# A transformer layer whose 1,450-word step table is written in a new order

## What is computed

```
mod = (silu(c) @ wmod)                      # six vectors of 256 for each batch element
h = layernorm(x) * (1 + ca) + sa
x = x + ga * attn(h)                        # 16 query heads in 4 groups, rope, causal softmax
h = layernorm(x) * (1 + cb) + sb
x = x + gb * ffn(h)

attn(h):  q, k, v = h@Wq+bq, h@Wk+bk, h@Wv+bv; scores = q k^T / sqrt(16), masked; y = softmax(scores) v
          return y @ Wo + bo                # the four query heads of a group are summed into one
ffn(x):   routed = sigmoid(x @ w_router + b_router) > 0.5
          h = x + (rmsnorm(x) @ wv + bv) @ wo
          mlp = (silu(h2 @ w_gate) * (h2 @ w_up)) @ w_down    # h2 = rmsnorm(h), 704 inner columns
          return where(routed, h + mlp, x)
```

## Time and profile before

| | us |
|---|---|
| median of three runs | 466.64 (465.21 to 467.13) |
| span of the profiled execution | 466.8 |
| TensorE busy | 437.2 (94%) |
| TensorE loading weights | 371.8 (80%) |
| VectorE busy | 353.9 (76%) |
| ScalarE busy | 308.4 (66%) |
| GpSimd busy | 182.2 (39%) |

### The profile page before, as it was taken

How to read it: one execution, slowest core, us unless ns; L and a number is a source line. 1 busy time by engine, 2 the same in 40 slices (tenths; PEclk the granted TensorE clock), 3 DMA queues, 4 the chain that set the end, 5 groups by cost and what they waited for, 6 DMA issues and landing times. The chain is left out here.

```text
span 466.8 us, 9486 instructions
## 1 busy us (share of the span) xinstructions
PE 437.2 (94%) x3320; PEld 371.8 (80%) x3320; DVE 353.9 (76%) x796; ACT 308.4 (66%) x640; POOL 182.2 (39%) x262
## 2 busy tenths in 40 slices
...
GB/s 192 333 93 51 3 97 1 2 1 3 0 3 11 43 2 0 2 70 1 27 86 24 2 1 24 1 26 5 20 51 9 24 22 2 25 1 24 22 25 46
DMA packets 16576, 16.04 MB, mean 34 GB/s; under 512 B 4233, under 2 KB 14926, under 8 KB 16530
## 3 DMA queue, kind: packets, MB, share of 16 engines
...
## 5 line engine op out<-in xcount | busy, mean ns | idle before, releaser
L792 PE MATMUL banks<-gTh,guhi 128*128 128x256 f32 x352 | 101.2, 287 | 0.0
L794 PE MATMUL banks<-gTh,gulo 128*128 128x256 f32 x352 | 98.8, 281 | 0.0
L793 PE MATMUL banks<-gTl,guhi 128*128 128x256 f32 x352 | 98.7, 280 | 0.0
L937 ACT ACTIVATE PT<-banks 128x1024 f32<-128x1024 f32 (+3 forms) x96 | 74.5, 810 | 29.8 <-PE banks L708 24.4
L792 PEld LDWEIGHTS banks<-gTh,guhi 128*128 128x128 f32 x352 | 66.4, 189 | 1.6 <-issue 0.7
L1165 DVE TENSOR_REDUCE mxp<-banks 128x2 f32<-128x1024 f32 (+3 forms) x56 | 61.9, 1141 | 6.4 <-PE banks L684 3.9
L793 PEld LDWEIGHTS banks<-gTl,guhi 128*128 128x128 f32 x352 | 66.5, 189 | 0.3
L794 PEld LDWEIGHTS banks<-gTh,gulo 128*128 128x128 f32 x352 | 66.4, 189 | 0.0
L684 PE MATMUL banks<-QKT 128*128 128x512 f32 (+3 forms) x192 | 49.9, 368 | 6.8 <-ACT QKT L915 3.4
L708 PE MATMUL banks<-QKT 128*128 128x512 f32 (+3 forms) x192 | 50.9, 369 | 0.9 <-ACT PT L937 0.4
L708 PEld LDWEIGHTS banks<-QKT 128*128 128x128 f32 x192 | 30.3, 190 | 23.3 <-issue 21.2
...
## 6 DMA issues: line engine op xcount, KB each, us to landing
...
```

What stands on the lines that cost most here:

```text
L792: pe.matmul(out_, guhi[:, k, blk, :], gh, start=(m == 0 and k == 0), stop=False)
L793: pe.matmul(out_, guhi[:, k, blk, :], gl, start=False, stop=False)
L794: i = pe.matmul(out_, gulo[:, k, blk, :], gh, start=False, stop=(m == len(blocks) - 1 and k == KB - 1))
L937: act.activation(PT[:, u % 2, 2 * q:2 * q + 2, 0:CH - q0], both("prob", b, n)[:, :, 0:CH - q0], ACT.Exp, scale=float(D) ** -0.5).then_inc( ...
```

## The change

Only the string `ORDER` differs. Its words are the same, as many of each, in another sequence, and TensorE words have other bank digits, which changes the waits for free banks. No instruction is added or removed. Of the table's 58 lines the first two:

```
-ldx ldx ldx ldx pzero asetw stats setw pmodc vmodc rstd1 norm1 norm1 xT4 xev qkv5 stats norm1 norm1 xT4 xev qkv4 asetb
-setb pmod amod rstd1 norm1 norm1 xT6 xev norm1 norm1 xT7 qkvb qkvb rope pprep0 afwv vkeys sthi qkv6 xev aprep pprep1
+ldx ldx ldx ldx pzero vkeys asetw stats pmodc setw rstd1 asetb norm1 stats norm1 norm1 xT4 norm1 vmodc xT5 setb rstd1
+xev qkv4 norm1 norm1 pmod xev qkvb norm1 norm1 pprep0 amod qkv5 afwv gmod xT4 qkvb xT3 xev rope qkv4 aprep pprep1
```

113 lines of the change are left out of this document (57 added, 56 removed).

## The result

The new order takes 471.99 us (470.19 to 474.56, 4 runs) against 466.44 (465.21 to 467.13): 1.0131 times the time before, 95% interval 1.0095 to 1.0166. I had forecast 464.5 us and a range up to 469.0.

A forecast was written before the change was run, and what follows sets the result against it. TensorE bounds it behind 160 us, VectorE's maxima from 36 to 60, cross-engine chains from 60 to 140. 466.8 + 0.0 (start) + 0.0 (maxima) - 2.5 (element 1) + 0.0 + 0.5 (full TensorE) - 0.3 (tail) = 464.5 us; range 461.0 to 469.0.

The forecast's parts named there:

- The base: Starting figure of the sum: the profiled 466.8 us, left uncorrected because span and median (466.64) differ by less than runs do.
- The start, 0.0: Up to the first `stack`: moving `vkeys` ahead wins and loses nothing; 0.0 us, bounds -0.5 and +1.0.
- does not take the first transposes before 13.62: At the start: the TensorE begins transposes only at 13.62, so it sees less of the 3.95 us delay; transposes 0.9 later.
- wrong if the first `stack` comes after 33 us: Sign set beforehand, at the start: a first `stack` later than 33 us would show the forecast wrong.
- Maxima of element 0, 0.0: Row maxima and what follows, up to 86 us: later `prob0.8` (+1.5) nearly all comes back; 0.0, bounds -1.0 and +1.5.
- Element 1, -2.5: From 86 us to element 1's maxima: shorter TensorE pauses, maxima at 98.0 instead of 100.52; -2.5 us, bounds -0.5 and -3.8.
- Where the TensorE is full, +0.5: Behind 160 us: too little TensorE work between some dependent steps makes pauses; +0.5 us, bounds -1.5 and +2.5.
- the four places that I named: Behind 160 us: pauses ahead of `prob2.8`, `prob2.0`, `yT2.0` and `up3.6`, 2.5 us, of which 0.5 was there before.
- The tail, -0.3: At the end: `fin3.2` begins 0.5 us earlier, out of the way of VectorE's L1286; -0.3 us.
- (A): Rival: element 1's whole chain (-3.8) and filled pauses (-1.2) count, nothing lost where TensorE is full; 461.8 us, chance 0.24.
- (B): Rival: VectorE takes up element 1's gain, and later `prob0.8` adds 1.5; 466.5 us, chance 0.20.
- (C): Rival: thin start lowers the clock (+1.7), late transposes +0.5, element 1's gain lost; 469.5 us, chance 0.14.

The follow-up runs named there:

- old_vfirst: The kernel before with one move alone, `vkeys` (three memsets on VectorE) put right behind `pzero`: 470.45 us, 1.0078 times the kernel before.
- old_light: The kernel before with GpSimd's `fin` steps (but the last pair's) and `ffl` from the third pair on cut to 8 columns, wrong values: 463.79 us, 0.9937.
- after_again: The changed kernel, unaltered, run once more for a second profile: 471.53 us, 1.0100 times the kernel before.

## Why the prediction was wrong, by its own steps

- **The base.** I set a span against a median of run times. A run takes 1.7 to 1.9 us more than its span, so the profile shown is of an execution of about 468.5 us, 1.9 above the median. Put right, the same sum gives 464.5 + 1.7 = 466.2 counted from that execution, but 466.4 - 2.3 = 464.1 counted from the median.
- **The start, 0.0: wrong, +5.7** to `stack0.0` by the medians of eight traces each (29.0 and 34.7), of which the maxima give 1.8 back, so +3.9. The first step that failed is that the TensorE "does not take the first transposes before 13.62". That is the profile's late `pmodc`; in the usual execution they start at 10.4 to 11.6, and `vkeys` ahead of them then costs what old_vfirst shows, 4.0 us. The second is "the first `stack` starts at about 31.7", followed along the TensorE's own queue through `pprep1`. In the new order `stack0.0` waits for VectorE's `stlo0.0`: `vkeys` (by way of `xT0.0`, 14.14) and `vmodc` (15.08) both keep `xev0.0` until 15.39, `pmod` holds `qkv0.1` (which the sum counted as a pause filled), and `rope0.0`, `qkvb0.2` and `stats1.0` follow. `stats0.0` came at 9.47 (forecast 9.8), `xT0.0` at 14.14 (14.5), `stack0.0` at 33.07 (31.7), and in the other traces of this front at 34.0 to 35.5; "wrong if the first `stack` comes after 33 us" was met.
- **Maxima of element 0, 0.0: better than forecast.** From `stack0.0` to `a0.0` the new order, with `vkeys` at the top, takes 48.3 to 48.6 us, the old one 50.1 to 50.5. `prob0.8` came late as traced, at 67.50 (67.2 to 67.4), and that cost nothing in the end.
- **Element 1, -2.5: right in sum, partly by luck.** -2.6 in every trace. `qkv1.3` started at 93.35 (forecast 92.7) and `max1.0` at 98.02 (98.0). But I took the maxima's gain as 98.0 against VectorE's 100.52, the start of a matmul against that of a reduction. The first reduction came at 99.39, 1.1 earlier; the gain up to `prob1.0` is 1.9, and 0.7 more falls between `prob1.0` and `down0.0`, which I had put at 0.0. TensorE timeline of after:

```profile
93.35 1.54 PE L663 MATMUL banks<-Wqkv,xTc 128*128 128x192 f32 x8
94.72 2.02 PE L673 MATMUL banks<-ident,stk 128*128 128x128 f32 x16
98.02 0.56 PE L684 MATMUL banks<-QKT 128*128 128x128 f32 x4
```

- **Where the TensorE is full, +0.5: wrong, +4.9** (the back's 4.5 without the tail). I weighed TensorE work against the length of chains and took each VectorE step at its usual length. Of the four places that I named only `prob2.8` shows the wait, 0.3 us; the waits that count end at VectorE. What I left out is how much VectorE and GpSimd work the new order puts side by side: between 283.5 and 326.4 us VectorE is busy for 38.0 of 42.9 us and GpSimd for 16.1, and with GpSimd's `fin` and `ffl` cut the loss of the back is gone.
- **The tail, -0.3: right.** L1286 takes 0.68 us instead of 1.55, and the last `sum` no longer waits for VectorE. From the start of the last matmul to it 0.31 us pass (464.11 to 464.42), before 0.72 (462.09 to 462.81); in all traces but old_light, whose GpSimd steps are cut, the last matmul's end lies 4.4 to 4.5 us before the end with the old tail and 4.0 to 4.1 with the new one. VectorE before and then after:

```profile
462.81 0.48 DVE L1278 SCALAR_TENSOR_TENSOR zbuf<-banks,r_yes,zbuf 128x256 f32<-128x256 f32 x1
```
```profile
464.42 0.48 DVE L1278 SCALAR_TENSOR_TENSOR zbuf<-banks,r_yes,zbuf 128x256 f32<-128x256 f32 x1 [0.38 <-PE banks L810]
```

- **The rivals.** (A) and (B) counted no loss at the start and at most 0.7 us in the back ((B)'s sum adds 0.7 where its text has 0.5). (C) named the right sign and half of the place: a late, thin start and a fall of the clock, 469.5 us. In after_again the clock is at half from 14.5 to 21.3 us; in the profile of after only from 11.0 to 14.4, ahead of the first transposes, and that execution is 1.8 us under the median. The two stretches, of after_again and then of after:

```profile
14.50:21.30 6.80, 6.34 (x26) 5.58 (x25) 1.34 (x10) 1.02 (x2) 4.22 (x9) 0.50 1.02 286
```
```profile
11.00:14.40 3.40, 3.10 (x15) 2.81 (x15) 2.35 (x12) 0.50 (x3) 2.82 (x6) 0.50 1.07 388
```

None of the rivals had the back, the larger loss.
